# A routed feed-forward kernel: one sort of all tokens into 19 tiles, or two halves of 11 tiles with the second half's attention and routing between the first half's tiles

## What is computed

```python
x = x + tanh(g_xattn) * attn(layernorm(x), ctx)   # sim = (ln(x) kv) kv^T * scale, layernorm over keys, softmax
h = layernorm(x)
scores = sigmoid(h @ gate_weight.T)               # 16 experts in 4 groups
# the 2 best groups by the sum of their 2 best (score + bias), in them the 4 best experts, weights normalised * 2.5
g, u = h @ gate_w[n].T, h @ up_w[n].T             # per expert n, 128 hidden features
routed = sum over chosen n of weight_n * (silu(g) * u) @ down_w[n].T
x = x + tanh(g_ffn) * (routed + shared_swiglu(h)) # the shared network has 256 hidden features
```

## Time and profile before

| | |
|---|---|
| time, median of 3 | 219.83 us |
| the profiled execution's own time | 218.19 us |
| its span, first to last instruction | 216.4 us |
| PE matmul busy | 163.0 us (75%), 1,080 instructions |
| DVE busy | 124.5 us (58%) |
| POOL busy | 90.3 us (42%) |
| ACT busy | 73.5 us (34%) |
| DMA | 17.94 MB, mean 83 GB/s |
| chain of waits that ended last | PE 59%, DVE 21%, POOL 6%, ACT 5%, DMA 5% |

### The profile page before, as it was taken

One profiled execution on the slowest core, in us unless ns is written; L12 is line 12 of the kernel. 1 busy time (PEld: TensorE's weight loads), 2 busy tenths in 40 slices (PEclk: granted clock), 3 DMA queues, 4 the chain that ended last, 5 costly groups with the idle time before them and its releaser, 6 DMA issues.

```text
span 216.4 us, 3728 instructions
## 1 busy us (share of the span) xinstructions
PE 163.0 (75%) x1080; PEld 144.0 (67%) x1080; DVE 124.5 (58%) x425; ACT 73.5 (34%) x207; POOL 90.3 (42%) x134
## 2 busy tenths in 40 slices
PE   7988712545494379829999999999999999999000
PEld 5744201533364267618999999999999999998000
DVE  1823289756899997622655655455654555544055
ACT  2758452332072131621334232333323342323000
POOL 5544344517365770880158333344334353111300
PEclk9999975555566555996999999999999999999855
DMA  6910203143515233311010121111121111100197
GB/s 147 366 77 0 74 3 121 51 121 83 183 26 191 83 97 113 83 50 33 0 55 26 53 74 49 55 53 35 38 61 59 52 53 50 51 26 27 27 295 274
DMA packets 10448, 17.94 MB, mean 83 GB/s; under 512 B 2715, under 2 KB 5788, under 8 KB 10430
## 3 DMA queue, kind: packets, MB, share of 16 engines
q1 hardware_dynamic: 5984, 11.27, 16.3%
q0 software_dynamic: 1824, 4.75, 7.4%
q10 hardware_dynamic: 2622, 1.69, 3.0%
HBM read 13.44 MB, written 4.65 MB: 84 GB/s over the span
## 4 chain that ended last, share of the span: by engine, by line
PE 59%; DVE 21%; POOL 6%; ACT 5%; DMA 5%; issue 2%; SPq 1%; POOLq 0%; ACTq 0%
PE bank L1032 25%; PE bank L1044 12%; POOL w_lo L256 5%; PE bank L997 5%; DVE col_hot L696 3%; PE bank L987 3%; PE bank L925 3%; DMA y_in<-pick_rows 2%; PE bank L975 2%; PE bank L1013 2%; DVE ln L545 2%; PE bank L1004 2%; DMA xg<-hid_rows,row_of 1%; PE bank L914 1%; ACT w_hi L356 1%
## 5 line engine op out<-in xcount | busy, mean ns | idle before, releaser
L256 POOL TENSOR_TENSOR w_lo<-w_raw,w_hi 128x256 fp32r<-128x256 f32 x54 | 38.2, 740 | 26.1 <-ACT w_hi L356 26.0
L741 DVE SCALAR_TENSOR_TENSOR act_f<-bank,w,silu_g 128x128 f32<-128x128 f32 x76 | 23.2, 346 | 41.6 <-ACT silu_g L408 41.5
L1032 PE MATMUL bank<-w_lo,g_hi 128*128 x152 | 43.1, 283 | 0.0
L1032 PE MATMUL bank<-w_hi,g_hi 128*128 x152 | 43.0, 283 | 0.0
L1032 PE MATMUL bank<-w_hi,g_lo 128*128 x152 | 43.0, 283 | 0.0
L408 ACT ACTIVATE silu_g<-bank 128x256 f32<-128x256 f32 x46 | 17.7, 385 | 60.3 <-PE bank L1032 60.2
L278 POOL DMA_INDIRECT pick_rows<-y_sb,pick_of x19 | 19.2, 1010 | 33.1 <-DVE y_sb L767 20.4
L271 POOL DMA_INDIRECT xg<-hid_rows,row_of x19 | 18.6, 981 | 34.2 <-DVE w L727 33.2
L1032 PEld LDWEIGHTS bank<-w_lo,g_hi 128*128 128x128 f32 x152 | 29.1, 192 | 0.0
L1032 PEld LDWEIGHTS bank<-w_hi,g_lo 128*128 128x128 f32 x152 | 29.1, 191 | 0.0
L1032 PEld LDWEIGHTS bank<-w_hi,g_hi 128*128 128x128 f32 x152 | 29.1, 191 | 0.0
(11 more groups left out here) (153 smaller groups left out, 325.4 us busy)
## 6 DMA issues: line engine op xcount, KB each, us to landing
w_raw<-w_in SPq DMA_DIRECT2D x18, 384.0 KB, 3.0
y_in<-pick_rows SPq DMA_DIRECT2D x8, 256.0 KB, 4.9
x<-x_in SPq DMA_DIRECT2D x4, 256.0 KB, 5.8
hid_rows<-ln ACTq DMA_DIRECT2D x4, 256.0 KB, 2.6
out<-x SPq DMA_DIRECT2D x8, 128.0 KB, 2.7
xg<-hid_rows,row_of POOLq DMA_INDIRECT x19, 2.8
pick_rows<-y_sb,pick_of POOLq DMA_INDIRECT x19, 2.4
cw<-ctxw_in ACTq DMA_DIRECT2D x1, 276.2 KB
```

The source lines that it names most:

```text
L256: nc.gpsimd.tensor_tensor(w_lo[:, n, cols], w_raw[:, n % RAW, cols], w_hi[:, n, cols].bitcast(F32), ALU.subtract).then_inc(w_lo_done, 1)
L741: ins = nc.vector.scalar_tensor_tensor(act_f[:, q % 2, e, :], halves[:, e, 1, :], w4[:, i % 2, 2 * h + e:2 * h + e + 1], silu_g[:, q % 2, ...
L1032: last = nc.tensor.matmul(gu_ps[q % 2][:, e * 2 * P:(e + 1) * 2 * P], m[:, i % 3, c, :], w[:, bass.ds(at + c * 2 * P, 2 * P)], start=j == ...
```

## The change

Tokens are sorted in two halves (batches 0 and 1, batches 2 and 3). Each half has 1,024 picks and at most (1024 + 4*127) // 128 = 11 tiles, so there are 22 in all. Steps of a half are 4 shared ones and 22 for its tiles: `QH` = 26. Attention up to the similarities is done for all batches first; the softmax of the second half, its residual, normalisation, routing, counts and lists are pieces placed behind steps 4 to 25 on each engine. Half 0's tiles run meanwhile. The results of half 0 are loaded back and added during the tiles of half 1.

The pieces need PSUM banks 6 and 7, so the gathered transposes (`tp_ps`) and the tile results (`y_ps`) have one bank each instead of two. ACT copies every tile's result (`y_copy`). The similarity matmul has no second, gamma-scaled copy of the keys; DVE centres and scales instead (`sim_stats`, `sim_centre`). Gathered transposes come one tile ahead. `FEW` = 4 is the tile before which all weights have to be complete; it was 8.

```diff
-PICKS = T * TOPK_GROUPS
+HTOK = HALF * P
+PICKS = HTOK * TOPK_GROUPS
 NTILE = (PICKS + GROUPS * (P - 1)) // P
-FEW = (PICKS - T) // P
+FEW = (PICKS - HTOK) // P
+QH = HALF + 2 * NTILE
...
-        gu_ps, at_ps, tp_ps, y_ps = bank[0:2], bank[2:4], bank[4:6], bank[6:8]
+        gu_ps, at_ps, tp_ps, y_ps = bank[0:2], bank[2:4], bank[4], bank[5]
...
@@ POOL @@
+            for b in range(B):
+                root(0, b)
...
+            low(0)
+            root(1, 0)
+            low(1)
+            root(1, 1)
+            low(2)
+            low(3)
+            root(2, 0)
+            root(2, 1)
+            for n in range(4, NF - EPG):
+                low(n)
+            for ti in range(XG):
+                gather(ti)
+            root(1, 2)
+            root(1, 3)
+            gather(XG)
+            gather(XG + 1)
+            ahead = XG + 2
+            for ti in range(2 * NTILE):
+                if ti == 2:
+                    root(2, 2)
+                if ti == 3:
+                    root(2, 3)
+                if ti < EPG // 2:
+                    low(NF - EPG + 2 * ti)
+                    low(NF - EPG + 2 * ti + 1)
...
+                scatter(ti)
...
@@ ACT @@
+            def y_copy(ti):
+                act.wait_ge(down_done, last_of(ti) + 1)
+                if ti >= YS:
+                    act.wait_ge(y_out[ti % YS], 16 * (ti // YS))
+                nc.scalar.copy(y_sb[:, ti % YS, :], y_ps[:, 0:D]).then_inc(y_done, 1)
+            def step(q):
+                silu(q)
+                if tile_of(q - 3)[1] == 1:
+                    y_copy(tile_of(q - 3)[0])
+                if q >= 1:
+                    act_high(q - 1)
+                if first_tile_of(q) is not None:
+                    gathered_high(first_tile_of(q))
+                ti, pair = tile_of(q)
+                if pair == 0 and ti % NTILE + 1 < NTILE:
+                    gathered_high(ti + 1)
...
+            high(11)
+            silu(3)
+            weight_rows(0)
+            high(12)
+            high(13)
+            act_high(2)
+            gathered_high(0)
+            between = {
+                5: [lambda: high(14)], 6: [lambda: softmax_exp(2), lambda: softmax_exp(3)], 7: [lambda: high(15)],
+                9: [lambda: high(16)], 11: [lambda: high(17)],
+                13: [lambda: hidden_high(2), lambda: hidden_high(3)], 17: [lambda: logit_exp(1)],
+                22: [lambda: weight_rows(1)],
+            }
...
@@ DVE @@
+            between = {
+                4: [lambda: sim_logits(2, 9)], 5: [lambda: sim_logits(3, 10)],
+                7: [lambda: residual(2)], 8: [lambda: x1_stats(2)], 9: [lambda: residual(3)], 10: [lambda: x1_stats(3)],
+                11: [lambda: normalise(2, 2, 11, hid, hid_ready)], 12: [lambda: normalise(2, 3, 12, hid, hid_ready)],
+                13: [lambda: hidden_low(2)], 14: [lambda: hidden_low(3)],
+                16: [lambda: add_logits(1)], 17: [lambda: score_groups(1)], 18: [rank_groups, lambda: pick_groups(1)],
+                19: [mask_groups], 20: [lambda: pick_experts(1), lambda: place_groups(1)],
+                21: [lambda: pick_weights(1), lambda: place_picks(1)],
+                22: [lambda: hot_tiles(0, NTK), lambda: hot_columns(0, HALF)],
+                23: [lambda: hot_columns(HALF, NTK)], 24: [lambda: list_rows(1)], 25: [lambda: tile_owners(1)],
+                QH + 10: [lambda: combine(0)], QH + 11: [lambda: combine(1)],
+                QH + 12: [lambda: combine(2)], QH + 13: [lambda: combine(3)],
+            }
...
@@ PE @@
+            def down(q, ti, pair):
                 pe.wait_ge(actlo_done, q + 1)
-                if i >= 2 and h == 0:
-                    pe.wait_ge((y_even_done, y_odd_done)[i % 2], i // 2)
+                if pair == 0:
+                    pe.wait_ge(pick_of_ready, ti // NTILE + 1)
+                    if ti >= 1:
+                        pe.wait_ge(y_done, ti)
...
+            def step(q):
+                ti, pair = tile_of(q)
+                any_gate_up(q)
+                if q >= 1:
+                    act_transposes(q - 1)
+                if pair == 0 and ti % NTILE + 1 < NTILE:
+                    gathered_transposes(ti + 1)
+                if q >= 2:
+                    any_down(q - 2)
+                if first_tile_of(q) is not None:
+                    gathered_transposes(first_tile_of(q))
...
+            between = {13: [lambda: hidden(2), lambda: hidden(3)], 15: [lambda: route(1)],
+                       19: [lambda: count_picks(1)], 24: [lambda: list_picks(1)]}
+            for q in range(HALF, 2 * QH):
+                step(q)
+                for piece in between.get(q, ()):
+                    piece()
```

More of the change, by code:

```diff
@@ new lines, in step @@
+            def step(q):
+                ti, pair = tile_of(q)
+                if ti is None:
+                    shared_mul(q)
+                else:
+                    act_mul(q, ti, pair)
+                if q >= 1:
+                    act_low(q - 1)
+                if first_tile_of(q) is not None:
+                    gathered_low(first_tile_of(q))
+                    tile_weights(first_tile_of(q))
+                if pair == 0 and ti % NTILE + 1 < NTILE:
+                    gathered_low(ti + 1)
+                if pair == 1 and ti % NTILE + 1 < NTILE:
+                    tile_weights(ti + 1)
+                if q >= 2 and shared_of(q - 2) is not None:
+                    shared_add(q - 2)
@@ L873, in _ @@
+            for q in range(HALF, 2 * QH):
+                step(q)
+                for piece in between.get(q, ()):
+                    piece()
+            act_low(2 * QH - 1)
+            for t in range(HALF, NT):
                 combine(t)
@@ L919, in similarity @@
                 pe.wait_ge(qT_ready, b + 1)
-                pe.wait_ge(keys_ready, b + 1)
-                pe.wait_ge(kvT_ready, B)
-                if b >= 2:
-                    pe.wait_ge(max_ready, b - 1)
-                for i, t in enumerate(tiles(b)):
-                    nc.tensor.matmul(sim_ps[t % 4][:, :], qT[:, b, i * P:(i + 1) * P],
-                                     keys[:, b].rearrange("k r s -> k (r s)"), start=True, stop=True)\
-                      .then_inc(sim_done, 1)
+                pe.wait_ge(kvT_ready, b + 1)
@@ L929, in hidden, with route @@
+                for i in range(2):
+                    last = nc.tensor.matmul(sim_ps[b][:, i * S:(i + 1) * S], qT[:, b, i * P:(i + 1) * P], kvT[:, b, :],
+                                            start=True, stop=True)
+                last.then_inc(sim_done, 1)
             def hidden(b):
-                if b < 2:
-                    pe.wait_ge(lnT_ready[b + 2], 1)
-                else:
-                    pe.wait_ge(hTlo_ready, b - 1)
+                pe.wait_ge(sim_read[b], 2)
                 transposes(b, hT_ps, hid, hid_ready, False).then_inc(hT_done, 1)
-            def route(b):
+            def route(h):
@@ L952, in count_picks @@
                                  start=True, stop=False, skip_group_check=True)
[L953 to L960 removed]
+                for t in range(HALF - 1):
+                    later = HALF - 1 - t
+                    nc.tensor.matmul(rank_ps[h][:, (t + 1) * GROUPS:n], ones_b[:],
+                                     own[:, t, :].unsqueeze(1).to_broadcast([P, later, GROUPS]),
+                                     start=False, stop=t == HALF - 2, skip_group_check=True)
@@ L961, in count_picks, with list_picks @@
+                for t in range(HALF):
+                    last = nc.tensor.matmul(rank_ps[h][:, n:n + GROUPS], ones_b[:], own[:, t, :],
+                                            start=t == 0, stop=t == HALF - 1, skip_group_check=True)
                 last.then_inc(ranks_done, 1)
-            def list_picks():
-                pe.wait_ge(tile_hot_ready, 1)
+            def list_picks(h):
+                pe.wait_ge(tile_hot_ready, h + 1)
                 for n in range(NTK):
-                    pe.wait_ge(col_hot_ready, n + 1)
-                    last = nc.tensor.matmul(list_ps[:, 0:NI], col_hot[:, n, :], tile_hot[:, n, :],
+                    pe.wait_ge(col_hot_ready, NTK * h + n + 1)
+                    last = nc.tensor.matmul(list_ps[h][:, 0:NI], col_hot[:, n, :], tile_hot[:, n, :],
@@ L1054, in _ @@
             project_transposed(1)
+            keep_warm(2, bank[7])
             pe.wait_ge(ident_ready, 1)
```

688 lines of the change are left out of this document (283 added, 405 removed).

## The result

The changed kernel takes 231.57 us (median of 4 runs, 230.28 to 231.84) against 220.02 us (219.82 to 220.72) for the kernel before, measured beside it: a ratio of 1.051, 95% interval 1.047 to 1.055. It is slower by 11.5 us. The forecast was 223.7 us with a range up to 228.5: the sign and most of the mechanisms were as forecast, the size was not.

The account below looks back on a forecast made before the run. PE bounds the tile steps, behind a chain across all engines. First tile at 61 us, steps, pieces and waits end the loop at 206.0; a 14.3 tail makes span 220.3, time 223.7 us (+1.8%), range 215.0 to 228.5.

Parts of the forecast that it names:

- single result bank: In pair-0 steps PE's down product waits for ACT's copy behind silu: 0.6 us in each of 20 tiles, 12.0 us.
- last weights: Before step 12 PE waits 2.9 us for the last weight blocks, plus 1.3 for roots on POOL: 4.2 us.
- exponentials: Second-half exponentials with table loads on ACT cost PE 2.1 us after step 6; at step 17 the spare covers them.
- DVE's pieces: Second-half work on DVE exceeds its free time at the counts (0.8) and in step 21 (1.2): 2.0 us.
- hand-over: The second half's first tile has its transposes only one step ahead: 1.2 us for the two parts.
- clock ahead of the first tile: PE idles some 8 us before the first tile, so the clock is low behind it: 2.2 us lost.
- where waits fall together: Overlapping waits in the loop were expected to take 1.5 us off the sum.
- tail: After the loop eight additions are left on DVE, and the last scatter starts 0.3 sooner: 14.3 us against 18.4.
- the front: Everything before the first sorted tile, mostly a straight line on DVE: the tile starts at 61 us, against 103.8.
- The pieces fit: Rival for steps 4 to 25: no waits from weights, exponentials and DVE, so 215.9 us; chance 0.25.
- The bank's wait is not there: Rival: ACT's copy is always done in time, 12 us go, giving 211.7 us; chance 0.03.
- The pile-up: Rival: waits in steps 7 to 21 also cost clock, table switches hold ACT longer: 227 to 229 us; chance 0.17.

Follow-up runs that it names:

- e1: Changed kernel with ACT's copy of a finished tile put ahead of silu in its step: 219.08 us, ratio 1.002 to the kernel before.
- e2: Changed kernel with the second half's softmax and routing exponentials computed as identities, so no table loads after the first silu: 227.1 us.
- e4: Changed kernel with the high parts of blocks 14 to 17 behind steps 4, 5, 8 and 9 on ACT, not 5, 7, 9 and 11: 225.65 us.
- e15: Changed kernel without the low parts of blocks 0 to 11 (small memsets on POOL instead; PE reads the high parts): 222.69 us, ratio 1.021 to the kernel before.
- e9: e8 with 28 extra unused matmuls on PE reaching up to the first sorted tile's transposes: 211.28 us, ratio 0.963 to the kernel before.
- e8: Changed kernel with three edits together: copy ahead of silu, last four high parts earlier, centred similarity in PSUM: 212.70 us, ratio 0.967 to the kernel before.
- e5: Changed kernel with the centred similarity kept in PSUM, so the logits pass reads PSUM instead of SBUF: 228.91 us, ratio 1.042 to the kernel before.
- e11: e8 with the exponentials written to PSUM, so the residual pass has one SBUF input: 210.84 us, ratio 0.961 to the kernel before.
- e7: Changed kernel with 16 extra unused matmuls on PE ahead of the first sorted tile's transposes: 232.0 us, median of three runs.
- e3: Changed kernel with the high parts of blocks 12 and 13 ahead of the weight rows' write on ACT: 230.20 us, ratio 1.054 to the kernel before.

## Why the prediction was wrong in size and right in mechanism

The changed kernel's own steps settle the sum. As a step without a wait I take 2.58 us for an even one and 2.37 for an odd one, as in e1, and 2.33 for a shared one. What a step has above that goes to the term whose work or wait lies in it; where two terms meet in one step, e1, e2 and e4 divide it.

| term | forecast | in the changed kernel's trace |
|---|---|---|
| start of the first sorted tile | 61.0 | 64.2 |
| 48 steps without waits | 118.7 | 118.1 |
| PE's pieces (steps 13, 15, 19, 24, 25) | 4.1 | 3.5 |
| single result bank | 12.0 | 15.3 |
| last weights, with the step behind (11, 12) | 4.2 | 4.9 |
| exponentials (8, 9, 18) | 2.1 | 4.4 |
| DVE's pieces (23) | 2.0 | 0.4 at most |
| hand-over (29, 30) | 1.2 | 1.5 |
| clock ahead of the first tile (4) | 2.2 | 1.4 |
| where waits fall together, and the rest | -1.5 | 0.4 |
| tail | 14.3 | 14.4 |
| span | 220.3 | 228.5 |

The steps of the prediction that failed are three sizes: the front (3.2 us too small), the result bank (3.3) and the exponentials (2.3), together 8.8 us where the span missed by 8.2. The other rows nearly cancel: the 1.5 taken off for waits that fall together was not there, and DVE's pieces and the clock cost less than forecast.

**The front: 61 forecast, 64.2 measured.** The step that failed here is "New for each batch are similarity statistics 1.1 and a centring pair 0.9 ..., with logits 1.6. That is 6.1 us a batch". The logits passes that I took the price from read PSUM, and the residual pair took 0.88 us from 33.84, when POOL made no low part. The change makes the logits pass read the centred copy in SBUF, and it and one residual pair now lie beside POOL's subtractions: 1.82 + 0.69 us in place of 1.6, and 1.78 for the pair. The end of the normalising passes was forecast at 28.6 and came at 31.8; e15 puts it at 27.4. I had written that small operations "are slower while POOL subtracts" and had left the large ones alone. That the front ends 3.2 us late, too, is partly chance: the pick weights ended 1.7 late (53.3 for 51.6), as the eight hot columns took 2.13 us where I had 3.5, and from the first gather to the first tile it was 5.2 us where I had 4.2.

**The single result bank: 12.0 forecast, 12.5 by e1, 15.3 in the steps.** The step that failed is "PE starts at about 141.27: 0.6 us late". It was right in its chain, but each wait was priced too low: a steady step lost 0.74 us (3.33 for 2.59), where I had 0.6, because PE starts 0.24 us behind the copy's end and not 0.1. Nineteen of the twenty lie in the loop. That e1 gave back only 12.5 is due to DVE's pieces: their 2.0 us were hidden behind the bank's wait, and 2.4 us of them came out in e1. So the number near 12 is partly luck.

**The last weights and roots: 4.2 forecast, 4.9 in the steps.** The mechanism and its place were right. The wait itself was 3.6 for 2.9, by the hand-over from POOL to PE; the roots for which 1.3 was counted stalled no step visibly; what the sum left out is the next step's clock (1.2).

**The exponentials: 2.1 forecast, 4.4 in the steps that e2 shortens.** The wait itself is near the forecast. The steps that failed are "PE loses 2.1" and, for the exponential at step 17, "which the spare covers". It was not covered: step 18 lost 1.2 us, since the next silu stood behind the load. About 1.0 us is the block of `high(15)` behind the late silu, and 0.3 to 0.4 the clock; both were in no term.

**Smaller terms.** Clock ahead of the first tile: 2.2 forecast, 1.4 in step 4, and 1.4 by e9 against e8. Hand-over: 1.2 forecast; the step has 1.0 us of wait for `g_lo` and lasts 3.71 us, and with the transposes one step earlier the two steps concerned fall by 0.6 (6.04 to 5.41). Tail: 14.3 forecast, 14.4 measured from the last down product of the steps.

**The rivals.** "The pieces fit" needed less than 2.9 us of waits; weights and exponentials alone made 9. "The bank's wait is not there" fails on 18 waits with ACT's copy as releaser. "The pile-up" (227 to 229) said that "each wait near 3 us in steps 7 to 21 may cost the clock": behind the wait of 3.6 us it did (0.65, 1.2 us), behind the exponentials it cost 0.3 to 0.4 us, and no table switch held ACT longer than its load. It came nearest in time and was given 0.17, but what filled the gap was mostly the front and the bank, which it did not name.

## What to carry to other kernels

When a change makes a pass read SBUF where it read PSUM, price it with what POOL does at that time, and keep the intermediate in PSUM if a bank is free; two such edits (e5, and e11 over e8) gave 2.7 and 1.9 us here. When buffers go from two to one, look at the order of the engine that empties the one left: two lines in ACT's list were worth what the whole change cost. And price a wait of PE with the step behind it, as a risk: behind the waits of 3.6 us the clock fell in every run here that kept it, behind those of about 1.6 us in two traces (the changed kernel and e7) and not in the others. A wait can also hide another one, which comes out when it is removed.

## What the runs showed that I had not expected

- A DVE operation of 128x32 elements took 0.77 us beside POOL's subtraction and 0.19 without; it waits for POOL's whole instruction. Leaving out POOL's front subtractions brought the first sorted tile forward by 8.4 us.
- Sixteen extra matmuls that ended 3.5 us before the real work brought no gain that showed, though they had raised the clock: it was back at 1.2 GHz as the first sorted step ran. Twenty-eight that reach up to it brought 1.4 us.
- Moving weights earlier in one list slowed another engine's chain by as much (e3): the first gather went out at 58.99 us in both.
